# Semaphores of TensorE raised on a drain behind the matmuls, in a three-layer graph network

## The chip, the cores and the metric

The kernel runs on one core of one Trainium2 chip. Times are device microseconds (us) of one execution. The engines are called TensorE (PE; its weight loads stand apart as PEld), VectorE (DVE), ScalarE (ACT), GpSimd (POOL) and SyncE (SP), as in the profile.

## The reference

6,250 nodes with 256 features, 100,000 edges sorted by destination, three relation types, three layers. Cut to what is computed:

```python
ew = edge_attr @ edge_w + edge_b                    # 100000 x 32 @ 32 x 256
inv_cnt = [1 / max(segment_sum(mask_r, dst), 1) for r in range(3)]
for l in range(3):
    residual = x
    msg = relu(x[src] * ew)
    out = sum(segment_sum(msg * mask_r, dst) * inv_cnt[r] @ weights[l, r] for r in range(3))
    out = out + x @ roots[l] + biases[l]
    x = residual + relu(out)
return layernorm(x_in + x)
```

## The kernel before, in words

The edges are cut into 782 tiles of 128. A step `q` handles two tiles, so a layer has 391 steps and the three layers 1,173. An order of the tiles is planned on the host side of the program (`plan()`), and with it the step at which each of the 49 blocks of 128 nodes has all its edges and can be multiplied by the layer's matrices.

For each tile GpSimd issues one indirect DMA (line 608) that gathers 128 rows of `x` into one of 12 buffers of the ring `xg`. It first waits on `s_sc` until TensorE has done with the pair of tiles that used the buffers before. For each step:

- `edge_weights` (line 781) makes the edge weights of two tiles in PSUM, four matmuls of 128x256, and raises `s_e` once.
- VectorE multiplies them into the gathered rows (line 1088, raises `s_m`), ScalarE applies relu (line 685, raises `s_r`).
- `collect` (line 800) multiplies the messages by one-hot selectors `S` (128x96 for each half of the features), eight matmul instructions, and raises `s_sc` once for each tile. In layer 0 two small bf16 matmuls (line 795) that count the edges stand before them.
- VectorE adds the two results into the accumulator (line 971, waits for `s_sc`, raises `s_acc`).

For each block of nodes TensorE turns the rows of `x` (`turn_x`, line 824, raises `s_xt`) and multiplies by four matrices (`mix`, line 849, four matmul instructions a call; the calls with m = 1 and 3 raise `s_d0` and `s_d1`). In layer 0 it also turns the edge attributes (`attr_turn`, line 754, raises `s_tr`) and takes differences of counts (`count`, line 812, raises `s_cm`).

The matmul instructions that an fp32 product is made of are counted as the profile counts them: two for each fp32 product, one for each product of `edge_weights`.

Of the kernel before, what the change touches and what calls it, by code (L numbers as in the profile page):

```python
# [59 lines left out]
def gnn_program(nc, x_in, src, dst, edge_attr, edge_type, weights, roots, biases, edge_w, edge_b, due, out):  # L60
# [19 lines left out]
    XB, XT, TB = 4, 2, 4  # L80
# [27 lines left out]
    with ctx:  # L108
# [17 lines left out]
        at = sb("at", [128, TR, 512], F32R)  # L126
        hs = sb("hs", [128, 3, 4, 64])
        W = sb("W", [128, 8, D])
# [3 lines left out]
        ident = sb("ident", [128, 128])  # L132
# [14 lines left out]
        xblk = sb("xblk", [128, XB, D])  # L147
# [25 lines left out]
        pE = bank[0:2]  # L173
        pA = bank[2:4]
        pT = bank[4]
# [544 lines left out]
        @block.tensor  # L720
        def _(eng):
            eng.wait_ge(s_id, 2)

            def turn(p, b0, b1):
                for c in range(CH):
                    q = 128 if c < CH - 1 else CL
                    b = b0 if c < 4 else b1
                    last = eng.transpose(b[:, 128 * (c % 4):128 * (c % 4) + q], c3(p)[0:q, c, :], ident[0:q, 0:q])
                last.then_inc(s_pt, 1)

            eng.wait_ge(s_pf, 1)
            turn(p_f, bank[0], bank[1])
            eng.wait_ge(s_pf, 2)
            turn(p_lo, bank[4], bank[5])
            eng.wait_ge(s_pf, 3)
            turn(p_rel, bank[2], bank[3])
            eng.wait_ge(s_idx, 2)
            eng.wait_ge(s_pf, 4)
            eng.wait_ge(s_cst, 2)
            for c in range(CH):  # L740
                eng.matmul(bank[c // 4][0:1, 128 * (c % 4):128 * (c % 4) + 128], base[:, c:c + 1], ident[:, :],
                           start=True, stop=True)
            eng.matmul(bank[1][0:1, 510:511], bad[:, 0:1], ones[:, :], start=True, stop=False)
            eng.matmul(bank[1][0:1, 510:511], bad[:, 1:2], ones[:, :], start=False, stop=True).then_inc(s_pt, 1)
            eng.wait_ge(s_pf, 5)
            turn(p_hb, bank[6], bank[7])
            turned = [0]

            def attr_turn(g):
                eng.wait_ge(s_lo, g + 1)  # L750
                eng.wait_ge(s_atc, g)
                eng.wait_ge(s_xc, turned[0])
                for i in range(tiles_of(g)):
                    last = eng.transpose(pT[0:64, 128 * i:128 * i + 128], hs[:, g % 3, i, :], ident[:, :])  # L754
                last.then_inc(s_tr, 1)

            eng.wait_ge(s_pca, 2)
            attr_turn(0)
            eng.wait_ge(s_pc, 2)
            eng.wait_ge(s_pca, 4)  # L760
            eng.wait_ge(s_wsb, 2)
            eng.wait_ge(s_one, 1)

            def edge_weights(l, q):
                Q = l * NP + q
                g = q // 2
                sl, times = ring(l, g, TR, NG)
                if q % 2 == 0:
                    if l == 0:
                        eng.wait_ge(s_atc, g + 1)  # L770
                    else:
                        eng.wait_ge(s_at[sl], 16 * (times - uses(1, sl, TR, NG)))
                if Q >= 2:
                    eng.wait_ge(s_m, Q - 1)
                if l and q == 0:
                    eng.wait_ge(s_f0, NB * l)
                    eng.wait_ge(s_f1, NB * l)
                for i in range(2):
                    c = 256 * (q % 2) + 128 * i
                    for p in range(2):  # L780
                        last = eng.matmul(pE[Q % 2][:, 256 * i:256 * i + 256], at[:, sl, c:c + 128],  # L781
                                          wsb[:, p, :], start=(p == 0), stop=(p == 1))
                last.then_inc(s_e, 1)

            def collect(l, q):
                V = l * NP + q
                eng.wait_ge(s_r, V + 1)
                if V >= 2:
                    eng.wait_ge(s_acc, 2 * (V - 1))
                eng.wait_ge(s_S, q // 2 + 1 + l * NQ)  # L790
                if l == 0:
                    eng.wait_ge(s_ob, q // 2 + 1)
                    eng.wait_ge(s_oh, 2 * V + 2)
                    for i in range(2):
                        eng.matmul(pA[V % 2][:, 384:384 + HW], oh_a[:, (2 * V + i) % AR, :],  # L795
                                   oh_b[:, slot(l, 2 * q + i), :], start=(i == 0), stop=(i == 1))
                for i in range(2):
                    n = 2 * V + i
                    for h in range(2):
                        last = eng.matmul(pA[V % 2][:, 192 * i + 96 * h:192 * i + 96 * h + 96],  # L800
                                          xg[:, n % XR, 128 * h:128 * h + 128], S[:, slot(l, 2 * q + i), :],
                                          start=True, stop=True)
                    last.then_inc(s_sc, 1)

            def count(k):

                if k == 0:
                    eng.wait_ge(s_df, 4)
                else:
                    eng.wait_ge(s_inv, 2 * k - 1)  # L810
                eng.wait_ge(s_cn, min(NP, starts[k] - 1))
                eng.matmul(pH[:, 4 * (k % 2):4 * (k % 2) + 3], diff[:, :], cnt[:, 3 * blocks[k]:3 * blocks[k] + 3],
                           start=True, stop=True).then_inc(s_cm, 1)

            def turn_x(l, k):
                K, n = NB * l + k, rows(k)
                eng.wait_ge(s_xl[K % XB], 16 * (K // XB + 1))
                if K:
                    eng.wait_ge(s_xc, K)
                if l == 0:  # L820
                    eng.wait_ge(s_atc, min(NG, turn_step(k) // 2 + 2))
                    turned[0] += 1
                for h in range(2):
                    last = eng.transpose(pT[:, 128 * h:128 * h + n], xblk[0:n, K % XB, 128 * h:128 * h + 128],  # L824
                                         ident[0:n, 0:n])
                last.then_inc(s_xt, 1)

            def mix(l, k, m):

                K, n = NB * l + k, rows(k)  # L830
                o = products(k, m)
                if k == NB - 1 and m == 0:
                    eng.wait_ge(s_m, (l + 1) * NP)
                if m == 0:
                    eng.wait_ge(s_xc, K + 1)
                if m == 0 and 0 < k < NB - 1:
                    eng.wait_ge(s_f0, K)
                if m == 0:
                    if k == 0:
                        eng.wait_ge(s_w, 80 * (l + 1))  # L840
                if m == 1:
                    eng.wait_ge(s_acc, l * NT + acc_by(k))
                if m == 2 and 0 < k < NB - 1:
                    eng.wait_ge(s_f1, K)
                for h in range(2):
                    r = m - 1
                    a = (acc[:, h, 384 * blocks[k] + r:384 * blocks[k] + r + 3 * (n - 1) + 1:3] if m
                         else xT[:, K % XT, 128 * h:128 * h + n])
                    last = eng.matmul(o, a, W[:, 2 * (r % 4) + h, :], start=(h == 0), stop=(h == 1))  # L849
                if m % 2:  # L850
                    last.then_inc(pair_done[m // 2], 1)

            pair_done = [s_d0, s_d1]
            def fast():
                for l in range(L):
                    for q in range(-3, end):
                        if 0 <= q + 1 < NP:
                            edge_weights(l, q + 1)
                        if l == 0:
                            for k in starting(q, 1):  # L860
                                count(k)
                        if 0 <= q - 1 < NP:
                            collect(l, q - 1)
                        for k in range(NB):
                            for m in range(R + 1):
                                if q == mix_step(l, k, m):
                                    mix(l, k, m)
                        if l == 0 and q % 2 and 1 <= (q + 3) // 2 < NG:
                            attr_turn((q + 3) // 2)
                        for k in range(NB):  # L870
                            if q == turn_step(k):
                                turn_x(l, k)

            both(eng, "tensor", fast)
# [266 lines left out]
```

## Time and profile before

| what | value |
|---|---|
| time, three runs | median 3587.23 us (3586.86 to 3590.75) |
| span of the profiled execution | 3632.0 us (the page gives no time of that execution beside its span) |
| mean granted TensorE clock | 0.895 of full speed |
| busy: PE, PEld | 2818.6 us, 2609.9 us (78%, 72%) |
| busy: POOL, DVE, ACT | 2256.5, 2148.2, 1285.0 us (62%, 59%, 35%) |
| matmuls, each with its weight load | 18,430 |

Busy time is the union of the recorded stretches of an engine. A matmul's record runs from its start to a modelled end, and records of neighbours overlap, so a busy PE is not one that could take no more. "Remote" as the releaser of a wait means that the profile has no event of this core that ends it.

### The profile page before, as it was taken

What the parts mean: (1) busy time and instruction counts of PE and PEld (TensorE: products, weight loads), DVE (VectorE), ACT (ScalarE), POOL (GpSimd) and SP (SyncE); (2) the same over time, 40 slices, a digit from 0 to 9 for tenths busy, and PEclk for the clock granted to TensorE, in tenths of its full rate; (3) what the DMA queues carried; (4) which work ended last, traced back from release to release, by engine and by line L of the source; (5) the groups of instructions that cost most, each with busy time, mean ns of one, the idle gap of its engine ahead of it and who ended that gap; (6) DMA issues with size and microseconds to landing.
All of it is one profiled execution on the core that took longest, in us unless ns stands there. A gap on an engine that the chain in (4) does not pass through costs nothing.

```text
span 3632.0 us, 59677 instructions
## 1 busy us (share of the span) xinstructions
PE 2818.6 (78%) x18430; PEld 2609.9 (72%) x18430; DVE 2148.2 (59%) x5997; ACT 1285.0 (35%) x2700; POOL 2256.5 (62%) x2368
## 2 busy tenths in 40 slices
PE   6777778888888777778777877777777777787777
PEld 5777777777777677777777777767666777777776
DVE  6666666666666555555555555545555665556566
ACT  6555555555555322222222222222222222222222
POOL 6666666666666466666666666646666666666664
PEclk9999999999999878888898888887888888888888
DMA  4444444444444344444444444434444444444443
GB/s 126 128 129 128 127 132 127 131 127 131 130 128 130 114 125 118 122 119 121 122 124 118 124 122 119 122 106 127 125 126 121 130 123 127 129 124 130 125 128 100
DMA packets 318631, 450.88 MB, mean 124 GB/s; under 512 B 155996, under 2 KB 205802, under 8 KB 318314
## 3 DMA queue, kind: packets, MB, share of 16 engines
q0 software_dynamic: 112608, 307.65, 29.8%
q1 hardware_dynamic: 205706, 139.36, 13.7%
q8 instruction: 156, 2.56, 0.3%
q14 instruction: 161, 1.32, 0.1%
HBM read 401.96 MB, written 44.82 MB: 123 GB/s over the span
## 4 chain that ended last, share of the span: by engine, by line
PE 61%; issue 16%; another core or an unknown queue 9%; DVE 8%; ACT 3%; DVEq 2%; POOL 1%; DMA 0%; POOLq 0%; SPq 0%
PE bank L800 31%; PE bank L781 14%; PE bank L849 13%; DVE acc L971 4%; PE bank L754 2%; DVE t L988 1%; DVE xg L1088 1%; ACT at L656 1%; PE bank L824 1%; ACT oh_a L702 1%; PE bank L795 1%; DVEq L1078 1%; DVEq L971 1%; DVE S L952 0%
## 5 line engine op out<-in xcount | busy, mean ns | idle before, releaser
L608 POOL DMA_INDIRECT xg<-x,idx x1564 | 1490.9, 953 | 897.3 <-issue 361.5
L800 PE MATMUL bank<-S,xg 128*128 128x96 f32 x9384 | 1459.0, 305 | 400.7 <-issue 197.4
L800 PEld LDWEIGHTS bank<-S,xg 128*128 128x128 f32 x9384 | 1324.2, 217 | 461.2 <-issue 441.2
L685 ACT ACTIVATE xg<-xg 128x512 f32<-128x512 f32 x1173 | 739.1, 630 | 2064.0 <-DVE xg L1088 1270.0
L971 DVE TENSOR_TENSOR acc<-acc,bank 128x192 f32 x2346 | 817.1, 348 | 767.0 <-PE bank L800 490.6
L1088 DVE TENSOR_TENSOR xg<-xg,bank 128x512 f32<-128x512 f32 x1173 | 802.0, 684 | 600.2 <-remote 273.5
L781 PE MATMUL bank<-wsb,at 128*128 128x256 f32 x4692 | 990.4, 338 | 213.8 <-issue 128.8
L608 POOL DMA_INDIRECT xg<-in_x_dram,idx x782 | 750.5, 960 | 451.0 <-PE bank L800 212.2
L781 PEld LDWEIGHTS bank<-wsb,at 128*128 128x128 f32 x4692 | 753.8, 214 | 286.7 <-issue 183.5
L849 PE MATMUL bank<-W,acc 128*128 128x256 f32 x1764 | 506.5, 411 | 2.2 <-issue 2.0
L849 PEld LDWEIGHTS bank<-W,acc 128*128 128x128 f32 x1764 | 385.5, 257 | 5.6 <-issue 2.0
L952 DVE TENSOR_TENSOR S<-iota,kr 128x384 f32<-128x384 bf16 x588 | 324.4, 552 | 0.2
L702 ACT ACTIVATE oh_a<-iota,lo 128x128 bf16<-128x128 bf16 x782 | 267.6, 389 | 69.3 <-PE bank L800 62.8
L988 DVE SCALAR_TENSOR_TENSOR t<-bank,inv,t 128x256 f32<-128x256 f32 x441 | 209.8, 476 | 19.2 <-remote 14.7
L849 PE MATMUL bank<-W,xT 128*128 128x256 f32 (+1 forms) x588 | 195.0, 464 | 0.0
L754 PE MATMUL bank<-ident,hs 128*64 128x128 f32 x782 | 126.1, 284 | 45.8 <-issue 40.4
L795 PE MATMUL bank<-oh_b,oh_a 128*128 128x12 bf16 x782 | 80.0, 174 | 101.1 <-issue 98.2
L795 PEld LDWEIGHTS bank<-oh_b,oh_a 128*128 128x128 bf16 x782 | 52.0, 105 | 132.3 <-issue 113.8
L849 PEld LDWEIGHTS bank<-W,xT 128*128 128x128 f32 (+1 forms) x588 | 125.7, 234 | 14.2 <-issue 0.3
L754 PEld LDWEIGHTS bank<-ident,hs 128*64 128x64 f32 x782 | 86.7, 122 | 58.0 <-issue 56.1
L656 ACT ACTIVATE at<-bank 64x512 fp32r<-64x512 f32 x196 | 113.1, 577 | 42.3 <-remote 32.7
L709 ACT ACTIVATE acc<-zcol 128x768 f32<-128x768 f32 (+1 forms) x98 | 81.7, 834 | 37.3 <-remote 21.7
(87 smaller groups left out, 728.2 us busy)
## 6 DMA issues: line engine op xcount, KB each, us to landing
at<-attr_t SPq DMA_DIRECT2D x390, 128.0 KB
xg<-x,idx POOLq DMA_INDIRECT x1564
attr_t<-at SPq DMA_DIRECT2D x195, 128.0 KB
xg<-in_x_dram,idx POOLq DMA_INDIRECT x782
hs<-in_edge_attr_dram SPq DMA_DIRECT2D x195, 64.0 KB
x<-t SPq DMA_DIRECT2D x96, 128.0 KB
xblk<-x SPq DMA_DIRECT2D x96, 128.0 KB
xblk<-in_x_dram SPq DMA_DIRECT2D x48, 128.0 KB
```

Of the source, the lines that this page charges most:

```text
L608: eng.indirect_dma_start(out=xg[:, n % XR, :], out_offset=None, in_=xs[l], in_offset=bass.IndirectOffsetOnAxis(ap=idx[:, tile(j):tile(j) + ...
L685: eng.activation(v, v, ACT.Relu).then_inc(s_r, 1)
L702: eng.activation(oh_a[:, j % AR, :], iota[:, 1:129], ACT.Sign, bias=lo[:, tile(j):tile(j) + 1]).then_inc(s_oh, 1)
L754: last = eng.transpose(pT[0:64, 128 * i:128 * i + 128], hs[:, g % 3, i, :], ident[:, :])
L781: last = eng.matmul(pE[Q % 2][:, 256 * i:256 * i + 256], at[:, sl, c:c + 128], wsb[:, p, :], start=(p == 0), stop=(p == 1))
L795: eng.matmul(pA[V % 2][:, 384:384 + HW], oh_a[:, (2 * V + i) % AR, :], oh_b[:, slot(l, 2 * q + i), :], start=(i == 0), stop=(i == 1))
L800: last = eng.matmul(pA[V % 2][:, 192 * i + 96 * h:192 * i + 96 * h + 96], xg[:, n % XR, 128 * h:128 * h + 128], S[:, slot(l, 2 * q + i), : ...
L849: last = eng.matmul(o, a, W[:, 2 * (r % 4) + h, :], start=(h == 0), stop=(h == 1))
L952: eng.tensor_tensor(S[:, at4:at4 + w, :], iota[:, 1:WK + 1].unsqueeze(1).to_broadcast([128, w, WK]), kr[:, c:c + w].unsqueeze(2).to_broadc ...
L971: eng.tensor_tensor(a, a, pA[V % 2][:, 192 * i:192 * i + 192] .rearrange("p (h w) -> p h w", h=2), ALU.add).then_inc(s_acc, 1)
L988: return eng.scalar_tensor_tensor(tt, products(k, m), inv[0:n, 3 * blocks[k] + r:3 * blocks[k] + r + 1], tt, ALU.mult, ALU.add)
L1088: eng.tensor_tensor(v, v, pE[Q % 2][:, :].rearrange("p (i d) -> p i d", i=2), ALU.mult).then_inc(s_m, 1)
```

## The change

In TensorE's main loop no matmul raises a semaphore any more. Each raise is put on a `drain` instruction that follows the matmuls on TensorE. `collect` raised `s_sc` by one behind each of its two tiles; it now raises it by two behind both.

```diff
@@ attr_turn
-                    last = eng.transpose(pT[0:64, 128 * i:128 * i + 128], hs[:, g % 3, i, :], ident[:, :])
-                last.then_inc(s_tr, 1)
+                    eng.transpose(pT[0:64, 128 * i:128 * i + 128], hs[:, g % 3, i, :], ident[:, :])
+                eng.drain().then_inc(s_tr, 1)
@@ edge_weights
-                        last = eng.matmul(pE[Q % 2][:, 256 * i:256 * i + 256], at[:, sl, c:c + 128],
+                        eng.matmul(pE[Q % 2][:, 256 * i:256 * i + 256], at[:, sl, c:c + 128],
                                           wsb[:, p, :], start=(p == 0), stop=(p == 1))
-                last.then_inc(s_e, 1)
+                eng.drain().then_inc(s_e, 1)
@@ collect
                     for h in range(2):
-                        last = eng.matmul(pA[V % 2][:, 192 * i + 96 * h:192 * i + 96 * h + 96],
+                        eng.matmul(pA[V % 2][:, 192 * i + 96 * h:192 * i + 96 * h + 96],
                                           xg[:, n % XR, 128 * h:128 * h + 128], S[:, slot(l, 2 * q + i), :],
                                           start=True, stop=True)
-                    last.then_inc(s_sc, 1)
+                eng.drain().then_inc(s_sc, 2)
@@ count
-                           start=True, stop=True).then_inc(s_cm, 1)
+                           start=True, stop=True)
+                eng.drain().then_inc(s_cm, 1)
@@ turn_x
-                last.then_inc(s_xt, 1)
+                eng.drain().then_inc(s_xt, 1)
@@ mix
                 if m % 2:
-                    last.then_inc(pair_done[m // 2], 1)
+                    eng.drain().then_inc(pair_done[m // 2], 1)
```

## Rows read from the trace of the kernel before

**Rows 1.** The page's first part: busy us (share of the span) and instructions.

```profile
PE 2818.6 (78%) x18430; PEld 2609.9 (72%) x18430; DVE 2148.2 (59%) x5997; ACT 1285.0 (35%) x2700; POOL 2256.5 (62%) x2368
```

**Rows 2.** The page's chain that ended last, by engine.

```profile
PE 61%; issue 16%; another core or an unknown queue 9%; DVE 8%; ACT 3%; DVEq 2%; POOL 1%; DMA 0%; POOLq 0%; SPq 0%
```

**Rows 3.** Groups of instructions: name, count | busy, mean ns | idle before, releasers.

```profile
L608 POOL DMA_INDIRECT xg<-x,idx x1564 | 1490.9, 953 | 897.3 <-issue 361.5 <-PE bank L800 254.5 <-remote 236.4
L800 PE MATMUL bank<-S,xg 128*128 128x96 f32 x9384 | 1459.0, 305 | 400.7 <-issue 197.4 <-DVE acc L971 194.1 <-DVE S L952 7.0
...
L781 PE MATMUL bank<-wsb,at 128*128 128x256 f32 x4692 | 990.4, 338 | 213.8 <-issue 128.8 <-DVE xg L1088 41.0 <-ACT at L656 28.5
...
L849 PE MATMUL bank<-W,acc 128*128 128x256 f32 x1764 | 506.5, 411 | 2.2 <-issue 2.0
...
L849 PE MATMUL bank<-W,xT 128*128 128x256 f32 (+1 forms) x588 | 195.0, 464 | 0.0
L754 PE MATMUL bank<-ident,hs 128*64 128x128 f32 x782 | 126.1, 284 | 45.8 <-issue 40.4 <-ACT xT L693 5.3
...
L824 PE MATMUL bank<-ident,xblk 128*128 128x128 f32 (+1 forms) x294 | 64.2, 304 | 23.2 <-issue 15.4 <-ACT at L656 7.7
...
L812 PE MATMUL bank<-cnt,diff 128*128 128x3 f32 x98 | 14.0, 213 | 0.0
```

**Rows 4.** Chain in order of time, 1813.5 to 1816.2 us: start, us, what.

```profile
1813.48 0.47 PE bank L781 x4
1813.95 0.86 PE bank L800 x8
1814.82 0.95 PE bank L849 x4
```

**Rows 5.** Line 781 from 1253 to 2420 us: ns, least, median and most.

```profile
L781 PE MATMUL bank<-wsb,at x1544: 274/282/776, 1252.7 to 2414.8; 128*128 128x256 f32 x193
```

**Rows 6.** Timeline, 1802.6 to 1809.7 us: start, us, instruction, [idle before, releaser].

```profile
1802.60 0.95 PE L781 MATMUL bank<-wsb,at 128*128 128x256 f32 x4
...
1804.76 1.03 PE L800 MATMUL bank<-S,xg 128*128 128x96 f32 x8
1805.52 0.95 POOL L608 DMA_INDIRECT xg<-x,idx  x1 [0.30 <-issue]
1808.04 0.69 DVE L1088 TENSOR_TENSOR xg<-xg,bank 128x512 f32<-128x512 f32 x1 [4.02 <-remote]
...
1808.30 0.94 POOL L608 DMA_INDIRECT xg<-x,idx  x1 [1.83 <-remote]
...
1808.85 0.53 PEld L781 LDWEIGHTS bank<-wsb,at 128*128 128x128 f32 x4 [3.22 <-issue]
1808.88 0.71 PE L781 MATMUL bank<-wsb,at 128*128 128x256 f32 x4 [3.09 <-issue]
```

**Rows 7.** Timeline, 34 to 36 us.

```profile
33.91 1.06 PE L754 MATMUL bank<-ident,hs 128*64 128x128 f32 x4
...
35.01 0.59 ACT L656 ACTIVATE at<-bank 64x512 fp32r<-64x512 f32 x1 [1.32 <-PE bank L754]
```

**Rows 8.** Waits over the whole run: us in total, times, longest us.

```profile
DVE acc L971 <- PE bank L800: 490.6, 298, 3.6
POOL xg L608 <- PE bank L800: 466.7, 409, 2.3
...
POOL xg L608 <- remote: 295.2, 185, 2.9
DVE xg L1088 <- remote: 273.5, 131, 4.6
DVE xg L1088 <- PE bank L781: 250.0, 134, 3.5
DVE acc L971 <- remote: 238.3, 117, 5.1
```

More of the change, by code:

```diff
@@ L823, in turn_x @@
                 for h in range(2):
-                    last = eng.transpose(pT[:, 128 * h:128 * h + n], xblk[0:n, K % XB, 128 * h:128 * h + 128],
+                    eng.transpose(pT[:, 128 * h:128 * h + n], xblk[0:n, K % XB, 128 * h:128 * h + 128],
                                          ident[0:n, 0:n])
-                last.then_inc(s_xt, 1)
+                eng.drain().then_inc(s_xt, 1)
             def mix(l, k, m):
@@ L848, in mix @@
                          else xT[:, K % XT, 128 * h:128 * h + n])
-                    last = eng.matmul(o, a, W[:, 2 * (r % 4) + h, :], start=(h == 0), stop=(h == 1))
+                    eng.matmul(o, a, W[:, 2 * (r % 4) + h, :], start=(h == 0), stop=(h == 1))
                 if m % 2:
-                    last.then_inc(pair_done[m // 2], 1)
+                    eng.drain().then_inc(pair_done[m // 2], 1)
             pair_done = [s_d0, s_d1]
```

## The prediction

> **What bounds the kernel now.** I read the page's busy line first [rows 1]: no engine is full. TensorE has the most, 2818.6 of 3632.0 us, at a mean granted clock of 0.895. The chain that ended last [rows 2] is 61% TensorE, 16% issue, 9% unknown and 8% VectorE. So the bound is a loop in which TensorE has the largest part and the other engines wait for it and it for them.
>
> How much could TensorE take? Where it runs without a wait, four instructions of line 781 take 0.47 us, eight of line 800 take 0.86 us and four of line 849 take 0.95 us [rows 4]. With the counts of [rows 3] (4692/4 = 1173 groups, 9384/8 = 1173, and (1764+588)/4 = 588) that is 551 + 1009 + 559 = 2119 us. The transposes and counts of lines 754, 824, 812 and 795 add about 140 us (their busy time less the tail of each group). Some 2,260 us at full clock, divided by 0.895 is 2,525 us. The span is 3,632 us, so TensorE has about 1,100 us in which it starts nothing. GpSimd needs 2,346 gathers of 0.953 us with 0.30 us of issue between them [rows 3, 6], 2,940 us; it isn't full either.
>
> Where does the rest go? In [rows 6] the four matmuls of line 781 that began at 1802.60 have their modelled end at 1803.55, and the multiplication that needs them begins at 1808.04, after 4.02 us of idle VectorE. Its gathers are no reason: by count they were issued around 1799 and 1800 us. Likewise line 800 ends at 1805.79 and GpSimd, free since 1806.47, gathers on at 1808.30. TensorE itself then stands for 3.09 us, because its next matmuls need that multiplication. At the start of the run it is otherwise: line 754 ends at 34.97 and ScalarE, which waits for it, begins at 35.01 [rows 7]. So in the steady stretch a semaphore of TensorE seems to come microseconds behind the modelled end of its matmul. [Rows 8] has the sum: VectorE waits 490.6 + 238.3 us at line 971 and 250.0 + 273.5 us at line 1088 for TensorE or for something that isn't shown, GpSimd 466.7 + 295.2 us. Whether the matmul really ends that late or only the raise is late is what the trace can't show. The change touches just this point, and that is why the range is wide.
>
> **The change part by part.** The drains: `edge_weights` 1173, `collect` 1173, `mix` 294 (two of four calls for each of 147 blocks), `attr_turn` 196, `turn_x` 147, `count` 49, together 3,032. No matmul is added or removed.
>
> What one drain costs on TensorE. Today matmuls of the next group start while the last ones of the group before are in flight. A matmul of line 781 has a record of 0.282 us [rows 5], but a new one starts about every 0.47/4 = 0.118 us [rows 4]. A drain gives up that overlap, 0.16 us. Then the next group has to start on an empty engine. No drain stands in the loop before; the nearest row is a start behind a semaphore: the multiplication ends at 1808.73, the weight load begins at 1808.85 and the matmul at 1808.88 [rows 6], 0.15 us. Together 0.31 us. A drain needs no crossing from another engine, so the restart can be shorter: with 0.04 us as from line 754 to ScalarE [rows 7] the price is 0.20 us. At the lower clock the part that is lost is longer (line 800 has a mean record of 305 ns against 0.108 us between starts [rows 3, 4]), so the upper end is 0.36 us. I take 0.25 us, nearer the low end, because a drain of the same engine resembles the prompt hand-over more. 3,032 times 0.25 is 758 us (0.20: 606; 0.36: 1,092).
>
> How much of it lies on the path. TensorE has 1,100 us free, so by room alone it all fits. But the free time is mostly the answer to TensorE's own lateness: VectorE waits for a group, and the next group waits for VectorE. A bubble inside such a loop lengthens it. I take the chain's share, between half and 61% [rows 2], of 758 us: 379 to 462 us, say 415. Queued behind each drain are the next group's waits and weight loads; the drain behind `edge_weights` holds back `collect` of two steps earlier, whose `s_sc` frees the gather buffers and lets line 971 go, and the drain behind `collect` holds back `mix` and the next `edge_weights`. With 606 and 1,092 us the same share gives 300 and 670 us.
>
> The single raise of `s_sc`: the first tile's sum can be added 0.43 us later (half of 0.86). Line 971 waits for both tiles anyway, the gathers wait for pairs, the selectors for whole pairs. In layer 0 ScalarE's one-hot (line 702) may wait for the odd tile: 391 times at most 0.43 us, and ScalarE is 35% busy, so its own slack covers it. I cost it at nothing; without that cover it is under 170 us.
>
> The Trainium skill, "TensorE: Matmul & The Clock Gate", "The cost: per-tile semaphore tail", has raises of concurrent matmuls serialize at 26.3 ns each. By that figure 1,173 raises fewer would give back 31 us, an estimate; no row here shows it, and the sum goes without it.
>
> The sum: 3587 + 415 is about 4,000 us. With the ends of the price it is 3,890 and 4,260 us. (Its terms come from an execution with a span of 3,632 us, 1.2% above the median of the runs; that moves a difference of 400 us by 5 us.)
>
> **The rivals.**
>
> *The raise on the drain is prompt, and the late raises are gone (the other side).* [Rows 6] speaks for it: if only the raise is late, a drain that raises from the sequencer may not share its path. Then the loops no longer stand for 3 to 4 us at a time, and TensorE becomes the bound: 2,525 + 758 = 3,280 us, with about 45 us before the loop and the turn of each layer, some 3,380 to 3,450 us. I give 3,440. It decides while the drain costs less than (3,540 - 2,525)/3,032 = 0.33 us. Against it: [rows 7] is prompt with the raise on a matmul, so the path isn't slow in itself; if the matmuls are really late under load, there is nothing to cure.
>
> *The bubbles are hidden and nothing else changes.* 758 us fit in the 1,100 us that are free, if TensorE's free time is not its own loop. The time would be 3,590 to 3,650 us. Against it stands TensorE's 61% of the chain [rows 2].
>
> *The drain waits out the lateness.* If the matmul itself completes 1 to 4 us after its modelled end, a drain holds TensorE for that long, where now the sequencer goes on issuing. One microsecond more at 2,346 drains, less the 1,100 us that are free, is over 1,200 us on top of 4,000: 5,200 us or more. Against it: the delays are longest where many groups are in flight, and drains would keep few in flight.
> The Trainium skill, "PSUM — Partial Sum Buffer", "Engine vs sequencer instructions", tells to attach the raise to the matmul and that a drain waits for the engine to go fully idle. That speaks for this rival and for the forecast; how long "fully idle" takes no row here shows.
>
> **How the numbers follow.** The forecast, drains that lengthen the loop (3,800 to 4,350 us), has 0.48; prompt raises (3,300 to 3,640) 0.25; hidden 0.17; waited out 0.10. The predicted time is 4,000 us. The range of 3,420 to 4,500 us leaves out the waiting-out and the lower part of the prompt case, together less than 0.2. What a measurement here can tell from no change is about 0.2%, 7 us. Faster: most of the prompt case and a little of the hidden one, 0.25; within 0.2%: 0.06 out of the hidden case; slower: 0.69.
>
> **What would show it.** In the page after: 3,032 drains, an idle time before the weight loads of lines 781 and 800 that is about 0.25 us a group, matmul starts that no longer reach back into the group before. If the forecast holds, VectorE's waits at lines 971 and 1088 for TensorE or unknown are not smaller than the 1,252 us of [rows 8], and the steps get longer evenly. If the prompt case holds, those waits shrink by more than half, the 3 to 4 us holes of [rows 6] are gone, and the chain is nearly all TensorE. If the waiting-out holds, single drains are recorded with more than 1 us. A drain price outside 0.20 to 0.36 us would make the sum wrong, and so would a change of the granted clock: at half speed a group takes nearly twice as long, so 0.05 less of clock would cost about 140 us.

## The result and the profile after

The changed kernel takes 4350.28 us (the mean of 4329.19 and 4371.37) against 3587.05 us (3586.80 to 3590.75): 1.2127 times the time, 95% interval 1.2066 to 1.2187, or about 763 us more. Two further runs of it, 4405.89 us (the profiled one) and 4413.15 us, took over 1.5% more than the fastest at a lower granted clock and stay out of this comparison. The forecast was 4,000 us; the median of all four runs is 4388.63 us.

The page of the changed kernel: busy line, then the chain by engine, as [rows 1] and [rows 2].

```profile
span 4404.2 us, 62709 instructions
...
PE 3546.4 (81%) x18430; PEld 2852.6 (65%) x18430; DVE 2277.2 (52%) x5997; ACT 1326.0 (30%) x2700; POOL 2245.4 (51%) x2368
...
PEld 52%; issue 30%; PEldq 15%; DVE 3%; ACT 0%; DMA 0%; DVEq 0%; POOL 0%; PE 0%; SPq 0%
```

There are 3,032 instructions more (62,709 less the 59,677 of before), all of them drains. The chain is now almost TensorE's alone: weight loads 52%, issue 30%, its sequencer (PEldq, where the drains are) 15%. VectorE has fallen from 8% to 3%, the unknown releaser from 9% to nothing. The mean granted clock is 0.829 in this run (0.850 and 0.861 in the two compared ones); before it was 0.895.

Its waits, as [rows 8]: us in total, times, longest us.

```profile
DVE acc L972 <- PEq L803: 994.8, 939, 7.5
DVE xg L1089 <- PEq L783: 543.2, 733, 4.0
```

Line 803 is the drain behind `collect`, 783 the one behind `edge_weights`. "Remote" is gone from this list: every wait for TensorE in the main loop ends at a drain that the trace shows. The total for VectorE is 1,538 us, where it was 1,252 us.

Its timeline at half and at full clock, as [rows 6].

```profile
2201.66 1.99 PE L800 MATMUL bank<-S,xg 128*128 128x96 f32 x8 [0.23 <-issue]
...
2203.80 0.36 DVE L972 TENSOR_TENSOR acc<-acc,bank 128x192 f32 x1 [1.53 <-PEq L803]
```

```profile
1886.45 1.10 PE L800 MATMUL bank<-S,xg 128*128 128x96 f32 x8 [0.23 <-issue]
1887.63 1.19 PE L850 MATMUL bank<-W,acc 128*128 128x256 f32 x4
1889.06 0.71 PE L781 MATMUL bank<-wsb,at 128*128 128x256 f32 x4 [0.23 <-issue]
1889.99 0.32 PE L800 MATMUL bank<-S,xg 128*128 128x96 f32 x1 [0.23 <-issue]
```

In the first fence the eight matmuls end at 2203.65 and VectorE starts on their sums at 2203.80. Before, line 800 ended at 1805.79 and VectorE's next sum began at 1808.65, and from the end of line 781 to its multiplication it was 4.5 us [rows 6]. The whole traces say the same. Take every step in which VectorE stood idle before its first sum, and count from the modelled end of that step's last matmul of line 800 to the start of the sum: before, the median is 3.24 us (446 cases), now 0.15 us (1,153 cases). The raises have become prompt.

In the second fence one sees what this costs at full clock: from the start of line 781 to that of line 800 it is 0.93 us where the chain had 0.47 us for the four matmuls [rows 4], and from line 800 to line 850 1.18 us in place of 0.86 us. That is 0.46 and 0.32 us, 0.39 us a drain on the mean. The split between single groups is rough, since without drains a group's first matmul starts beside the last ones of the group before; over a whole round this drops out. The three groups from line 800 to line 800 take 3.54 us (1886.45 to 1889.99), and in [rows 4] 2.28 us, 0.42 us for each of the three drains.

### The profile page after: what moved, and what is told of

Read it like the earlier page. It is cut to its first block, busy times and chain, and to the rows that moved or that the text cites. A ratio compares the mean times of both kernels' runs of the same rounds, so it can differ in the third digit from the quotient of the medians.

```text
span 4404.2 us, 62709 instructions
## 1 busy us (share of the span) xinstructions
PE 3546.4 (81%) x18430; PEld 2852.6 (65%) x18430; DVE 2277.2 (52%) x5997; ACT 1326.0 (30%) x2700; POOL 2245.4 (51%) x2368
## 3 DMA queue, kind: packets, MB, share of 16 engines
q0 software_dynamic: 112608, 307.65, 24.7%
## 4 chain that ended last, share of the span: by engine, by line
PEld 52%; issue 30%; PEldq 15%; DVE 3%; ACT 0%; DMA 0%; DVEq 0%; POOL 0%; PE 0%; SPq 0%
PEld bank L800 25%; PEld bank L781 14%; PEld bank L850 9%; PEldq L803 5%; PEldq L783 4%; PEldq L852 1%; PEld bank L795 1%; PEld bank L754 1%; PEldq L790 1%; DVE acc L972 1%; PEldq L755 1%; PEldq L774 1%; PEld bank L825 1%; DVE xg L1089 1%; DVE S L953 1%
## 5 line engine op out<-in xcount | busy, mean ns | idle before, releaser
L800 PE MATMUL bank<-S,xg 128*128 128x96 f32 x9384 | 1564.0, 319 | 276.5 <-issue 220.3
L800 PEld LDWEIGHTS bank<-S,xg 128*128 128x128 f32 x9384 | 1381.5, 226 | 439.0 <-issue 428.4
L781 PE MATMUL bank<-wsb,at 128*128 128x256 f32 x4692 | 1043.1, 353 | 223.2 <-issue 162.0
L781 PEld LDWEIGHTS bank<-wsb,at 128*128 128x128 f32 x4692 | 788.7, 227 | 483.1 <-issue 444.6
L608 POOL DMA_INDIRECT xg<-in_x_dram,idx x782 | 740.8, 947 | 695.6 <-PEq L803 569.6
L850 PE MATMUL bank<-W,acc 128*128 128x256 f32 x1764 | 595.1, 467 | 42.7 <-issue 9.6
L850 PEld LDWEIGHTS bank<-W,acc 128*128 128x128 f32 x1764 | 403.6, 266 | 131.6 <-issue 117.0
L850 PE MATMUL bank<-W,xT 128*128 128x256 f32 (+1 forms) x588 | 220.7, 512 | 48.8 <-issue 48.8
L996 DVE TENSOR_TENSOR t<-bank,bias 128x256 f32<-128x256 f32 (+1 forms) x147 | 62.4, 425 | 128.5 <-PEq L852 101.7
L754 PEld LDWEIGHTS bank<-ident,hs 128*64 128x64 f32 x782 | 74.5, 115 | 76.3 <-issue 74.3
```

What stands on the lines that cost most here:

```text
L608: eng.indirect_dma_start(out=xg[:, n % XR, :], out_offset=None, in_=xs[l], in_offset=bass.IndirectOffsetOnAxis(ap=idx[:, tile(j):tile(j) + ...
```

## The experiments

The questions left by the result: what a drain costs, whether the lateness was of the raise or of TensorE, and where it came from. Two theories stood at first. One: only a raise on a matmul is late, and each takes its turn. The other: TensorE itself is behind its recorded ends, so that a drain has to wait as well.

### One raise in place of two

```diff
-                    last.then_inc(s_sc, 1)
+                last.then_inc(s_sc, 2)
```

> The kernel before, with s_sc raised once by two on the last matmul of collect; no drain. If each raise on a matmul takes its turn in a slow path (the kernel before raises about 4,200 times in 3,587 us), 1,173 raises fewer shorten the waits and the time falls by 3 to 10%, to 3,230 to 3,480 us. If the lateness has to do with the matmuls in flight or with the gathers and not with the number of raises, the time stays within 1% of 3,587 us.

3584.18 us, ratio 0.999 (0.998 to 1.0). 1,173 raises fewer gave 3 us. The number of raises is not what makes them late, and the merging of the two raises of `s_sc` has no part in the 763 us.

### Drains on one kind of raise only

```diff
-                    last.then_inc(s_sc, 1)
+                eng.drain().then_inc(s_sc, 2)
```

> The kernel before, with s_sc alone on a drain (1,173 of the 3,032 drains). If a drain costs 0.39 us of TensorE, as the starts across it in the changed kernel show (508 ns against 118 ns), these cost 457 us of issue; if they also make all raises prompt, the time is 3,350 to 3,650 us. If drains only cost and cure nothing, it is 3,587 plus 38% of the 801 us, 3,890 us.

3737.06 us, ratio 1.042 (1.0403 to 1.0438). It lies between the two cases, and neither was right: the drains cost less than a bubble of 0.39 us each (128 ns each in time). Either they give something back, or part of them lies where TensorE stood idle anyway; this run doesn't tell which.

```diff
-                last.then_inc(s_e, 1)
+                eng.drain().then_inc(s_e, 1)
```

> The kernel before, with s_e alone on a drain (1,173 drains); s_sc is raised twice on matmuls. If the cost is by the drain, the time is that of the run with the drain on s_sc within 2%. If the raise that matters is s_sc, which frees the gather buffers and the sums, this one is slower than that run by over 2%.

4091.4 us, ratio 1.1424 (1.1387 to 1.1461): as many drains, over three times the price, 0.43 us each. The place matters. The drain behind `edge_weights` stands in front of `collect`, which frees the gather buffers and hands the sums to VectorE. The granted clock was 0.815, against 0.883 with the drain behind `collect`. No run separates the clock. An estimate from the runs of the changed kernel, which took 84 us less at a clock of 0.861 than at 0.826 (24 us for each 0.01), puts some 160 us of the 354 us between the two kernels down to it.

### The drains without the raises

```diff
-                eng.drain().then_inc(s_e, 1)
+                last.then_inc(s_e, 1)
+                eng.drain()
```

(and so for all six kinds)

> All 3,032 drains of the changed kernel, but they raise nothing; the raises stay on the last matmul before each (s_sc once by two). If the price is the drain itself, the time is that of the changed kernel (4,330 to 4,410 us) within 2%. If it is the path of the raise, it differs: slower, 4,800 us or more, where the drain waits for a late raise; and the waits for TensorE tell whether raises on matmuls are still late when few matmuls are in flight.

4408.64 us, ratio 1.2286 (1.2235 to 1.2338), within 2% of the changed kernel, as expected. The intervals of the two ratios don't meet, but the difference goes with the granted clock. This kernel took 4393 us at 0.830 and 4424 us at 0.823; the changed kernel took 4406 us at 0.829, 4413 us at 0.826, 4371 us at 0.850 and 4329 us at 0.861. At nearly the same clock the two agree within 0.3%. Whether the place of the raise has a part in the clock isn't shown. The waits, as those above:

```profile
DVE acc L977 <- PE bank L802: 926.8, 912, 2.3
DVE xg L1094 <- PE bank L782: 493.0, 702, 2.5
```

The raises are on matmuls here, and the waits end at those matmuls and are as in the changed kernel. From the modelled end of line 802 to VectorE's first sum, counted as above, the median is 0.13 us. So a raise on a matmul isn't late in itself. The path of the raise is worth nothing that these runs can tell from the clock; what the change did, it did by emptying TensorE at each of the 3,032 places. The first theory fell with this run.

### Fewer drains

```diff
                     last.then_inc(s_sc, 1)
+                if q % 2 == 1:
+                    eng.drain()
```

> The kernel before with a drain that raises nothing behind collect in every second step, 586 drains; all raises stay on matmuls. If a drain is only a bubble of 0.39 us, they cost up to 229 us and each ends about 0.02 us behind the last modelled matmul end. If TensorE is really behind its recorded ends in a long stream, these drains end later than those of the run with one drain a step (there a median of 0.13 us and a quarter over 0.78 us), 1 us or more. The time is then 3,590 to 3,750 us; under 3,560 us if an occasional drain cures more than it costs.

3697.42 us, ratio 1.032 (1.0302 to 1.0338).

Then the same in every fourth step (`q % 4 == 3`):

> The same with a drain in every fourth step, 291 drains. If TensorE's arrears are bounded, the drains end 2 to 4 us behind the last modelled end and the time is within 2% of 3,587 us; if a drain is only a bubble, they end 0.02 us behind it and the time is at most 3,700 us.

3662.67 us, ratio 1.022 (1.0184 to 1.0256). 586 drains cost 111 us, 291 cost 76 us: the fewer they are, the more one costs (0.19 and 0.26 us; 0.13 us in the run with 1,173 behind `collect`). That fits drains that wait until an engine in arrears has caught up, and the ends of the drains show it directly. The median drain ends 0.02 us behind the last modelled end of a matmul in the changed kernel, 0.11 us with 1,173 drains, 0.98 us with 586 and 1.41 us with 291 (a tenth of these over 3.8 us). The last is less than the 2 to 4 us that were expected. So TensorE itself is behind its recorded ends, and not only the raise; that is the second theory. The groups of line 849 and of its line in the changed kernel, 850, show the same: weight loads with count, busy, mean, idle before. First the run with drains behind `collect` alone, then the changed kernel.

```profile
L849 PEld LDWEIGHTS bank<-W,acc 128*128 128x128 f32 x1764 | 386.3, 258 | 289.7 <-issue 273.6 <-DVE acc L971 11.2
```

```profile
L850 PEld LDWEIGHTS bank<-W,acc 128*128 128x128 f32 x1764 | 403.6, 266 | 131.6 <-issue 117.0
```

Before these loads stands a drain in both, but where the other drains are missing the engine is idle in the records for 290 us there, and for 132 us where every group is drained. In the records TensorE has finished; by the drain it hasn't. None of these runs with drains is faster than the kernel before.

### What puts TensorE in arrears

[Rows 7] has a hint. Where the raise was prompt, GpSimd was writing zeros; its gathers of the loop begin later:

```profile
32.73 4.05 POOL L622 MEMSET acc<- 128x4736 f32 x1
...
36.94 0.96 POOL L608 DMA_INDIRECT xg<-in_x_dram,idx  x1 [0.15 <-issue]
```

First the gathers were taken out; GpSimd writes a constant instead, and the messages are made of it in place of the nodes' rows.

```diff
-                eng.indirect_dma_start(
-                    out=xg[:, n % XR, :], out_offset=None, in_=xs[l],
-                    in_offset=...).then_inc(s_g[n % XR], 16)
+                eng.memset(xg[:, n % XR, :], 0.5).then_inc(s_g[n % XR], 16)
```

> The kernel before without its gathers: GpSimd writes 0.5 into each buffer and raises s_g in place of the indirect DMA, so the messages are wrong and GpSimd needs under 0.5 us a tile. If the traffic of the gathers makes TensorE late, the waits for TensorE nearly vanish and the time falls to 2,600 to 3,000 us. If the stream of matmuls itself does it, the time stays over 3,300 us and the waits are still there.

2443.65 us, ratio 0.6816 (0.6802 to 0.6829), less than the 2,600 us expected at the least. All of TensorE's 18,430 matmuls are still there. Page and waits of this run:

```profile
PE 2369.7 (97%) x18430; PEld 2294.2 (94%) x18430; DVE 2159.6 (88%) x5997; ACT 1277.2 (52%) x2700; POOL 679.6 (28%) x2368
...
PE 93%; DVE 3%; issue 2%; DMA 1%; DVEq 0%; ACT 0%; SPq 0%
```

```profile
DVE acc L969 <- PE bank L798: 43.7, 186, 1.0
...
DVE xg L1086 <- PE bank L779: 21.6, 25, 7.0
```

TensorE is busy for 97% of the span, at a clock of 0.995, and raises on its matmuls are prompt: at these two lines VectorE waits for it 65 us where it waited 1,252 us, and the median from modelled end to first sum is 0.13 us. So a dense stream alone doesn't do it; the gathers do.

Not all of the 1,143 us between the two kernels is TensorE's lateness. 2,346 gathers of 0.953 us with 0.30 us between them are 2,940 us of GpSimd by [rows 3, 6], an estimate: with all gathers a kernel can't be faster than that, however prompt TensorE is. About 500 us of the difference are GpSimd's own pace; some 650 us are left for the lateness and for the lower clock that came with it.

Three runs ask what of a gather holds TensorE up.

Plain loads of as many bytes, from ScalarE's queue:

```diff
+                                eng.wait_ge(s_sc, 2 * ((n - XR) // 2 + 1))
+                                eng.dma_start(xg[:, n % XR, :], xs[l][a:a + 128, :]).then_inc(s_g[n % XR], 16)
```

> The kernel before, but each tile's 128 rows come by a plain load of consecutive rows from ScalarE's queue (from SyncE's for the first 12), so the messages are of the wrong nodes; the same bytes, GpSimd issues nothing. If it is the data traffic into the buffers that makes TensorE late, waits for TensorE over 0.5 us stay and the time is over 3,300 us. If it is GpSimd's indirect DMA, the time comes near the 2,444 us of the run without gathers, up to 2,900 us.

2470.09 us, ratio 0.6809 (0.6789 to 0.6829). Here the messages are made of real rows, if of other nodes, so the constant of the run before wasn't what made it fast.

The same plain loads, issued by GpSimd (in place of the gather, with `a = (j * 8) % (N - 128)`):

> The same plain loads of consecutive rows, but issued by GpSimd. If what matters is that GpSimd writes the descriptors, this is as slow as the kernel before (3,400 to 3,700 us) and TensorE is late; if only the indirect form does it, it is under 2,900 us.

2462.8 us, ratio 0.6789 (0.6756 to 0.6822). Its page, the busy line, the queue's, and the group of one of the loads:

```profile
PE 2379.3 (96%) x18430; PEld 2304.3 (93%) x18430; DVE 2160.8 (88%) x5997; ACT 1277.2 (52%) x2700; POOL 1263.0 (51%) x2368
...
q0 software_dynamic: 112608, 307.65, 43.7%
...
L609 POOL DMA_DIRECT2D xg<-x x1564 | 831.6, 536 | 719.3 <-PE bank L799 662.5
```

These are the same 112,608 packets and 307.65 MB on the same queue as before, and TensorE is 96% busy. Neither the amount of traffic nor the queue is the cause. The rows are consecutive here and scattered in the gather, though.

The indirect DMA with 32 bytes a row:

```diff
-                    out=xg[:, n % XR, :], out_offset=None, in_=xs[l],
+                    out=xg[:, n % XR, 0:w], out_offset=None, in_=src_rows,   # w = 8
```

> The kernel before, but from the 13th on a gather brings 32 bytes a row in place of 1 KB (the messages are wrong): GpSimd issues as many indirect DMAs with as many rows and 1/32 of the bytes. If GpSimd's issue and the descriptors matter, the time stays within 5% of 3,587 us; if the bytes matter, it falls under 3,000 us.

3630.79 us, ratio 1.0011 (1.0 to 1.0022; the kernel before took 3,627 us on that chip). Groups and waits of this run:

```profile
L610 POOL DMA_INDIRECT xg<-x,idx x1564 | 1495.1, 956 | 889.2 <-issue 369.1
```

```profile
DVE acc L973 <- PE bank L802: 427.5, 275, 3.9
```

11 MB in place of 308 MB on that queue, and nothing changes: 0.956 us an issue, TensorE late as before (median 3.20 us). What counts is the indirect form on GpSimd, 0.95 us an issue against 0.54 us for the plain one, and not its bytes. Whether it's the form or the scattered addresses wasn't separated: no run has indirect DMAs of consecutive rows.

Then half of the tiles by the indirect DMA and half by plain loads:

```diff
+                if n % 4 < 2:
                     eng.indirect_dma_start(...)
+                else:
+                    eng.dma_start(xg[:, n % XR, :], xs[l][a:a + 128, :]).then_inc(s_g[n % XR], 16)
```

> The kernel before with two of every four tiles brought by the indirect DMA as before and two by GpSimd's plain loads of consecutive rows (wrong messages for those). If each indirect DMA holds TensorE up by its own share (1,124 us for 2,346 of them, 0.48 us each), half of them cost half: about 3,025 us. If it is their density that fills a queue, the time is nearer one end: under 2,700 us, or over 3,400 us.

2475.71 us, ratio 0.6905 (0.6885 to 0.6925). Half of them cost next to nothing, so the hold-up isn't so much for each issue. The group of the gathers in layers 1 and 2, and a wait over the whole run:

```profile
L609 POOL DMA_INDIRECT xg<-x,idx x782 | 792.5, 1013 | 278.0 <-issue 174.4
```

```profile
DVE acc L975 <- PE bank L804: 96.5, 198, 1.4
```

GpSimd is in indirect issues for about 48% of this run's span (1,174 x 1.01 us of 2,474 us), against 62% before (2,346 x 0.955 us of 3,632 us), and here at most two follow each other. Also, GpSimd's own pace is no bound here: it is busy for 1,877 us of the 2,474 us. The lateness is nearly gone as well (median 0.18 us, a tenth over 1.35 us). Which of the three makes the difference wasn't tried.

### The price of the drains without the gathers

This is the changed kernel, with GpSimd writing the constant in place of the gathers.

> The changed kernel with its 3,032 drains, without gathers as in the run above that took 2,444 us (wrong messages again). There TensorE is 97% busy, so every drain should cost its full bubble: 3,032 times 0.39 us is 1,182 us, 3,626 us, if the clock stays near full. If the drains cost 0.25 us it is 3,200 us. If it is slower than 3,700 us, the clock has fallen.

3768.21 us. Against the 2443.65 us of the same kernel without drains that is 1,325 us for 3,032 drains, 0.437 us each (two chips; the kernel before differed between them by 1.1%, and by the ratios to it, 1.0388 and 0.6816, it would be 1,281 us, 0.42 us each). It is over the 3,626 us that were expected for 0.39 us a drain, and over the 3,700 us that were to show a fallen clock; the clock was 0.975 and 0.952 in its two runs, after 0.995. Its chain in order of time shows one more place where the excess over 0.39 us goes:

```profile
2203.36 0.98 PEldq L801
...
2204.46 0.36 DVE acc L970
```

After the drain behind `collect` (line 801) the chain goes over to VectorE, which can only now add the sums, and comes back to TensorE later. Without the drains VectorE's work lay beside the matmuls.

## Why the prediction was right or wrong

**What bounds the kernel.** The reading that the steady stretch holds TensorE up by microseconds, and that the start of the run doesn't, was right. That the gathers of the multiplication at 1808.04 were no reason was right too, but by count they were issued at 1795.07 and 1796.48, not around 1799 and 1800 us. TensorE's own time, 2,260 us at full clock, was some 4% short: without gathers it is busy for 2,370 us at a clock of 0.995. The share of the chain was taken for a fixed loop; it was in part TensorE's own arrears under GpSimd's indirect issues, and in part GpSimd's pace.

**The count of drains,** 3,032, was right.

**The price of a drain** was mis-sized, and it is the largest miss of the sum: 0.25 us, with 0.36 us as the upper end, where the rows of the changed kernel show 0.39 us at full clock and the pair of runs without gathers 0.42 to 0.437 us in time. The overlap given up was right in kind; the restart was taken too short. The hand-over from line 754 to ScalarE [rows 7] is that of a prompt raise to another engine; that TensorE's next group has its own waits, weight load and first matmul to bring up would explain the rest, but no run takes these apart. The row of a start behind a semaphore (0.15 us) was the better one and still too low. The idle PE time that shows it is 0.23 us before a group; with the 0.16 us of overlap it makes the 0.39 us.

**The share on the path** was near as a number and wrong in its reason. Half to 61% of the price was to lie on the path, because the chain had that share. The 763 us are 58% of 1,325 us and 65% of 3,032 times 0.39 us. But with drains TensorE is 97% of the chain, and without gathers the whole price shows in the time. It isn't that 40% of each drain was hidden by a loop that stayed as it was; the loop changed.

**What was left out of the sum:** the drains also take the place of something. With gathers they cost 763 us and not 1,281 to 1,325 us, some 520 to 560 us less. The pages show where: TensorE's busy time grew by 728 us with gathers and by 714 us without, but its idle time grew by 45 us with gathers (from 813 to 858 us) and by 598 us without (from 72 to 670 us). The idle time at the drains replaced an idle time that was there before. This is the mechanism of the rival that the late raises are gone, and it came about: "remote" vanished and VectorE starts a median of 0.15 us behind the modelled end. How much of the old idle time was the lateness and how much GpSimd's pace isn't separated. But it came with the full price, and it isn't by the path of the raise, as that rival had it: the run with drains that raise nothing has it too. The rival's own limit, 0.33 us a drain, is passed by the 0.39 us. The signs were mixed: VectorE's waits at the two lines grew to 1,538 us, as the forecast had it, and the chain became nearly all TensorE, as the rival had it.

By the prediction's own terms 415 us were expected and 763 us measured; it is 1,325 less 562 us, where the prediction had 758 us by 0.55. That the time fell into the range with a price outside its bounds is in part luck: the idle time that the drains replaced wasn't in the sum.

**The hidden case** is refuted, and so is the waiting-out at its price of 5,200 us. Its sign, drains recorded with more than 1 us, did appear, but it is no sign of it. These are the records of the drains behind `collect` in the changed kernel, in ns, least, median and most:

```profile
L803 PEldq DRAIN  x1173: 930/1138/8260, 33.8 to 4384.8; - x196
```

Such a record begins while the matmuls in front still run; the median drain ends 0.02 us behind their modelled end. In the runs with few drains the case's kind can be seen: the arrears are waited out there.

**The clock** was named as what would make the sum wrong. It fell from 0.895 to 0.850 and 0.861 in the compared runs. At 24 us for each 0.01, as the changed kernel's own runs have it, that is some 100 us of the 763 us, an estimate; the prediction's 140 us for 0.05 was about right. Without gathers the drains took it from 0.995 to 0.975 and 0.952.

**The rule of the Trainium skill,** "PSUM — Partial Sum Buffer", "Engine vs sequencer instructions", to attach the raise to the matmul: these runs agree. Both are as prompt as the engine lets them be, and the drain costs 0.39 us. The 26.3 ns a raise of the Trainium skill, "TensorE: Matmul & The Clock Gate", "The cost: per-tile semaphore tail", which the page has for tiles that run at once, would have given 31 us for 1,173 raises, an estimate; the run with one raise gave 3 us.

**What stays open.** Why indirect issues on GpSimd hold TensorE up, whether it is their form or their scattered rows, and whether their share of time, their sequence or GpSimd's own pace makes the difference between one half and all of the tiles. A version that gives all gathers and spares TensorE wasn't found: 2,346 issues of 0.95 us and 0.30 us between them are 2,940 us in themselves. No kernel here that makes all the gathers in full beat the one before by more than 0.1% (0.999 with one raise).

## What to carry to other kernels

A drain on TensorE isn't a cheap way to raise a semaphore: it costs the overlap of two groups and a restart, 0.39 us here with groups of 0.5 to 0.9 us, and here it made TensorE the chain although it had been idle for 22% of the span. Where an engine's consumers start microseconds after its modelled ends, first ask what else runs at that time, by taking other engines' work out one at a time; how the semaphore is raised may be beside the point. And an engine's free time is no cover for a cost until it is known why it is free.

## What the runs showed of the hardware that was not expected

- TensorE's stream of 18,430 matmuls with their weight loads takes 2,444 us without indirect DMAs and 3,587 us with 2,346 of them issued by GpSimd, although not a matmul differs. Plain loads by GpSimd with the same bytes and packets take 2,463 us, indirect ones with 1/32 of the bytes 3,631 us, half of each kind 2,476 us. About 500 us of the first difference are GpSimd's own pace.
- Under these issues a matmul's modelled end is no sign that what waits for it can start: a median of 3.24 us lay between them at line 971, against 0.13 us without gathers and 0.14 us with plain loads.
- A drain shows such arrears: with 291 of them the median one ends 1.41 us behind the last modelled end, with 3,032 of them 0.02 us.
- The kernel's dependence on the place of the drain: 1,173 drains behind `collect` cost 150 us, as many behind `edge_weights` 504 us.
